# A recurrent block and a rounded feed-forward layer on one core: rounding of weights by adding transfers, maxima taken later, transfers in the planner

## What is computed

```
u = layernorm(x) @ W_in.T + b_in                      # 512 -> 1024
s[t] = tanh(u[t] + s[t-1] * gamma + beta)             # 1024 steps, one after another
x = x + layernorm(s @ W_out.T + b_out)                # 1024 -> 512
h = layernorm(x)
q(w) = w.astype(float8_e4m3fn).astype(float32)
gate = silu((h @ q(gate_w)) * gate_scale)             # 512 -> 1536
up = (h @ q(up_w)) * up_scale
x = x + layernorm(((gate * up) @ q(down_w)) * down_scale)   # 1536 -> 512
```

## Time and profile before

| | us |
|---|---|
| median of 3 runs | 600.39 (599.93 to 606.07) |
| the profiled execution | 603.18 |
| its span, first to last instruction | 601.4 |
| first scan starts | 21.07 |
| last scan starts | 539.14 |
| busy: PE, DVE, ACT, POOL | 557.9, 398.2, 325.5, 208.7 |

### The profile page before, as it was taken

How to read it: one execution, slowest core, us unless ns; L and a number is a source line. 1 busy time by engine, 2 the same in 40 slices (tenths; PEclk the granted TensorE clock), 3 DMA queues, 4 the chain that set the end, 5 groups by cost and what they waited for, 6 DMA issues and landing times.

```text
span 601.4 us, 10100 instructions
## 1 busy us (share of the span) xinstructions
PE 557.9 (93%) x2984; PEld 467.4 (78%) x2984; DVE 398.2 (66%) x1638; ACT 325.5 (54%) x1496; POOL 208.7 (35%) x335
## 2 busy tenths in 40 slices
PE   4999798899899999999999999999999997988993
PEld 4766465789779887988788988988798786876992
DVE  3987967778686666766685758665666677655213
ACT  2765564655557554755466545755575555551330
POOL 1100214356637232534244314432233233521622
PEclk9999899899999999999999999999999998999998
DMA  8774114001012001010012001200010000200000
GB/s 267 212 243 143 53 44 150 1 19 36 1 36 71 1 1 36 14 58 2 1 36 71 1 1 36 71 2 1 1 41 32 1 1 2 71 1 1 37 0 35
DMA packets 16598, 27.47 MB, mean 46 GB/s; under 512 B 2336, under 2 KB 4512, under 8 KB 16544
## 3 DMA queue, kind: packets, MB, share of 16 engines
q1 hardware_dynamic: 16544, 26.84, 13.9%
HBM read 22.63 MB, written 4.19 MB: 45 GB/s over the span
## 4 chain that ended last, share of the span: by engine, by line
DVE 35%; PE 32%; ACT 21%; issue 5%; DMA 4%; POOL 1%; SPq 1%; POOLq 0%; DVEq 0%; ACTq 0%
DVE recur L934 17%; ACT pairs L1215 12%; PE gate_up L854 11%; PE wide L811 6%; DVE fused L1050 5%; PE wide L880 4%; ACT pairs L1202 4%; PE wide L789 4%; ACT gated L1238 3%; PE wide L765 3%; ACT fused_hi L1254 2%; PE wide L898 1%; DVE x_norm L1024 1%; DVE z L1062 1%; DVE y L974 1%
## 5 line engine op out<-in xcount | busy, mean ns | idle before, releaser
L934 DVE TENSOR_TENSOR_SCAN recur<-recur,pairs 128x32 f32<-128x32 f32 x1024 | 235.7, 230 | 139.8 <-ACT pairs L1215 139.5
L1215 ACT ACTIVATE pairs<-recur 128x16 f32<-128x16 f32 x1024 | 191.8, 187 | 211.3 <-DVE recur L934 206.6
L811 PE MATMUL wide<-w_out_sb,pairs 128*128 128x512 f32 x256 | 116.0, 607 | 10.0 <-ACT pairs L1215 9.8
L1325 POOL TENSOR_TENSOR fused_lo<-fused,fused_hi 128x256 fp32r<-128x256 f32 x96 | 72.0, 750 | 145.6 <-ACT fused_hi L1254 145.5
L811 PEld LDWEIGHTS wide<-w_out_sb,pairs 128*128 128x128 f32 x256 | 74.7, 298 | 44.4 <-ACT pairs L1215 9.5
L789 PE MATMUL wide<-x_norm_t,w_in_sb 128*128 128x256 f32 x448 | 102.7, 386 | 6.3 <-ACT x_norm_t L1170 3.2
L854 PE MATMUL gate_up<-x_hi,gate_q 128*128 128x256 f32 x384 | 103.3, 301 | 4.4 <-DVE x_lo L1035 4.4
L789 PEld LDWEIGHTS wide<-x_norm_t,w_in_sb 128*128 128x128 f32 x448 | 85.1, 193 | 21.8 <-ACT x_norm_t L1170 6.3
L854 PE MATMUL gate_up<-x_lo,up_q 128*128 128x256 f32 x384 | 97.3, 286 | 0.0
L854 PE MATMUL gate_up<-x_hi,up_q 128*128 128x256 f32 x384 | 96.9, 285 | 0.0
L854 PE MATMUL gate_up<-x_lo,gate_q 128*128 128x256 f32 x384 | 96.5, 284 | 0.0
(11 more groups left out here) (93 smaller groups left out, 563.7 us busy)
## 6 DMA issues: line engine op xcount, KB each, us to landing
x_in<-x SPq DMA_DIRECT2D x16, 256.0 KB, 3.2
x_res<-x SPq DMA_DIRECT2D x16, 256.0 KB, 3.3
out<-z SPq DMA_DIRECT2D x14, 256.0 KB, 3.6
w_in_sb<-w_in_t SPq DMA_DIRECT2D x4, 512.0 KB, 5.6
w_out_sb<-w_out_t SPq DMA_DIRECT2D x8, 256.0 KB, 5.1
raw_own<-gate_w SPq DMA_DIRECT2D x6, 256.0 KB, 5.9
raw_own<-up_w SPq DMA_DIRECT2D x6, 256.0 KB, 4.2
z<-down_w SPq DMA_DIRECT2D x6, 256.0 KB, 3.0
```

Of the source, the lines that this page charges most:

```text
L811: ins = eng.matmul(wide[b][:, :], pairs_by_batch[:, state_slots(n, b), :, j, 0].rearrange("p s b -> p (s b)"), w_out_sb[:, j, :], start=(j ...
L934: eng.tensor_tensor_scan(preact.rearrange("p c k -> p (c k)"), factors.rearrange("p c k -> p (c k)"), pairs[:, (t - 1) % RING, :, :].rearr ...
L1215: eng.activation(pairs[:, t % RING, :, 0], preact[:, :, 1], ACT.Tanh).then_inc(s_state, 1)
L1325: eng.tensor_tensor(fused_lo[:, f, :], fused[:, f, :], fused_hi[:, f, :].bitcast(F32), ALU.subtract).then_inc(s_fused_lo, 1)
```

## The change

- The planner gets a fifth resource, `dma`, on which loads of pieces, of x, of the scale rows and of W_out take their turn (1.5 steps per 256 KB, landing 7 steps later). `ENGINE_FREE` says from when each resource is free; conversions of all 36 pieces are planned, none by hand.
- Twelve pieces (9, 13, 17, 21 and 28 to 35) are rounded by transfers that add: POOL issues one that adds the constants to the raw row, ACT writes the negated constants into the weight's place (`negate_constants`, two halves), and POOL issues a second that adds the raw row to it. The other 24 go through PE as before. POOL itself adds nothing any more.
- The maxima are taken of the rounded pieces, planned from step 60 on and at the lowest rank.
- Early pieces have nine raw rows (two of `x1_norm` more) and six rows of constants (two in `x1_lo`).
- In the head PE makes 4 products of zeros once DVE has cleared two rows of `fused`; the first u goes to four banks in parts of two columns of 128, and each part is copied by itself.

```diff
+ISSUE_STEPS, LOAD_STEPS, LOAD_LANDS = 1.0, 1.5, 7.0
+ADD_ISSUE_STEPS, SETTLE_ISSUE_STEPS, SUM_STEPS, SUM_LANDS = 2.2, 1.9, 3.0, 6.0
+ENGINE_FREE = {"tensor": -4.0, "vector": -18.0, "scalar": -1.5, "gpsimd": -20.0, "sync": -24.0, "dma": -9.5}
+DOWN_RANK, NEGATE_RANK, ISSUE_RANK, PEAK_RANK, FIRST_X1_RANK = 20.0, 0.0, -2.0, 150.0, -4.0
+PEAKS_FROM = 60.0
+WARM_PRODUCTS = 4
...
+def by_transfer(i):
+    return i >= 28 or i in (9, 13, 17, 21)
...
+    def load(name, after, parts=1):
+        t.add("sync", name, ISSUE_STEPS * parts, after, 0.0)
+        t.add("dma", ("landed", *name), LOAD_STEPS * parts, [(name, 0.0)], 0.0)
+        return [(("landed", *name), LOAD_LANDS)]
...
+            side("vector", ("constant", i), [(("power", i), 0.0)] + (unrounded(j) if j is not None else []), k - 1,
+                 two_ports=True)
+            if by_transfer(i):
+                for h in range(2):
+                    side("scalar", ("negate", i, h), [(("constant", i), 0.2)] + behind("negate", ("negate", i, h)),
+                         NEGATE_RANK + 0.01 * i)
+                t.add("gpsimd", ("add", i), ADD_ISSUE_STEPS,
+                      [(("constant", i), 0.2)] + behind("add", ("add", i)), ISSUE_RANK, no_ports=True)
+                t.add("dma", ("summed", i), SUM_STEPS, [(("add", i), 0.0)], 0.0)
+                t.add("gpsimd", ("settle", i), SETTLE_ISSUE_STEPS,
+                      [(("summed", i), SUM_LANDS)] + [(v, 0.2) for v in pair("negate", i)]
+                      + behind("settle", ("settle", i)), ISSUE_RANK, no_ports=True)
+                t.add("dma", ("settled", i), SUM_STEPS, [(("settle", i), 0.0)], 0.0)
...
             for h in range(2):
+                side("vector", ("peak", i, h), done(i) + behind("peak", ("peak", i, h)) + [(peaks_from, 0.0)], PEAK_RANK + 0.01 * i)
...
         raw = [raw_own[:, r, :] for r in range(OWN)] + [z[:, b, :] for b in range(batch)] + [
-            x_res[1][:, b, :] for b in range(batch)]
+            x_res[1][:, b, :] for b in range(batch)] + [x1_norm[:, b, :] for b in range(batch)]
+        rounders = [rounders_own[:, r, :] for r in range(NR)] + [
+            x1_lo[:, b * KD // 2:(b + 1) * KD // 2, :].rearrange("p k t -> p (k t)") for b in range(batch)]
...
-        for i in range(FIRST_PIECES):
-            at["raw", i] = HEAD + 20 + i
-            at["power", i] = HEAD + FIRST["pieces"] + 4 * i
...
+                eng.wait_ge(s_blank, 1)
+                for _ in range(WARM_PRODUCTS):
+                    eng.matmul(round_banks[0], fused[:, 0, 0:P], fused[:, 0:2, :].rearrange("p f t -> p (f t)"),
+                               start=True, stop=True)
...
+                for m in range(MS):
+                    yield HEAD + FIRST["first_u"][m]
+                    if m == 0:
+                        eng.wait_ge(s_x_norm_t, 1)
+                    eng.wait_ge(s_w_in_in[m], 16)
+                    for jj in range(2):
+                        j = 2 * m + jj
+                        for k in range(KD):
+                            ins = eng.matmul(wide[m][:, jj * P:(jj + 1) * P],
+                                             w_in_sb[:, k, j * P:(j + 1) * P], x_norm_t[:, k, 0:P],
+                                             start=(k == 0), stop=(k == KD - 1))
+                    ins.then_inc(s_u_psum, 1)
...
+                        wait_constant_read(eng, before)
...
+                        eng.mul(pieces[i][1][:, halves(h)], rounders[rounder_of[i]][:, halves(h)].bitcast(F32),
+                                -1.0).then_inc(s_negated, 1)
...
+                    yield at["add", i]
+                    eng.wait_ge(s_raw_in[raw_of[i]], 16 * (raw_use[i] + 1))
+                    eng.wait_ge(s_constant, i + 1)
+                    eng.dma_start(raw[raw_of[i]], rounders[rounder_of[i]].bitcast(F32),
+                                  accum_op=ALU.add).then_inc(s_summed[raw_of[i]], 16)
...
+                    yield at["settle", i]
+                    eng.wait_ge(s_negated, 2 * transfer_pieces(i + 1))
+                    eng.wait_ge(s_summed[raw_of[i]], 16 * sums_into_raw(i))
+                    eng.dma_start(pieces[i][1], raw[raw_of[i]], accum_op=ALU.add).then_inc(s_settled[raw_of[i]], 16)
```

More of the change, by code:

```diff
@@ L75, in lay @@
     def lay(self):
[L78 removed]
+        open_jobs = {e: [] for e in ENGINE_FREE}
         for name, job in self.jobs.items():
@@ L88, in lay @@
         begin, running = {}, []
-        free = {e: -60.0 for e in open_jobs}
+        free = dict(ENGINE_FREE)
         shared_until, pool_until = -60.0, -60.0
@@ L266, in converted, with read, unrounded @@
+    def read(i):
+        return [(("settled", i), SUM_LANDS)] if by_transfer(i) else [(("round", i), 0.3)]
+    def unrounded(i):
+        if by_transfer(i):
+            return [(("summed", i), SUM_LANDS)] + [(v, 0.2) for v in pair("negate", i)]
+        return [(("round", i), 0.3)]
     def converted(pieces):
[L267 removed]
+        return [v for i in pieces for v in done(i)]
     def weights():
[L271 to L296 removed]
@@ L297, in weights @@
[L297 to L310, removed]
@@ L311, in weights, with behind @@
-        for step in range(4):
-            before = [("peak", i, h) for i in range(FIRST_PIECES, NP) for h in range(2)] if step == 0 else [("guard", step - 1)]
-            side("vector", ("guard", step), [(v, 0.0) for v in before] +
-                 ([(v, 0.3) for v in done(NP - 1)] if step == 3 else []), 180)
+        before = {}
+        def behind(strand, name):
+            after = [(before[strand], 0.0)] if strand in before else []
+            before[strand] = name
+            return after
@@ new lines, in weights @@
+        for step in range(4):
+            after = [(v, 0.0) for v in pair("peak", NP - 1)] if step == 0 else [(("guard", step - 1), 0.0)]
+            side("vector", ("guard", step), after + (done(NP - 1) if step == 3 else []), PEAK_RANK)
+    x_landed = {1: load(("x_load", 1), [(-18.0, 0.0)], parts=batch)}
+    rows_landed = load(("rows",), [(2.0, 0.0)], parts=3)
+    w_out_landed = []
+    for j in range(KH):
+        w_out_landed += load(("w_out", j), [(W_OUT_FROM + W_OUT_EVERY * j, 0.0)])
@@ L331, in next_x @@
     def next_x(n):
-        norm_x(n, [(("t1", n - 1, b), 8.0) for b in range(batch)], rank(n - 1, 10) if n > 2 else X2)
+        x_landed[n] = load(("x_load", n), [(("t1", n - 1, b), X_BEHIND if n < 4 else 0.3) for b in range(batch)], parts=batch)
+        norm_x(n, x_landed[n], rank(n - 1, 10) if n > 2 else X2)
     next_x(2)
@@ L368, in timetable @@
             if p == 0 and i == 2:
-                after += converted(i for i in range(NP) if not by_pool(i))
+                after += converted(i for i in range(NP) if not by_transfer(i))
             for b in range(batch):
```

263 lines of the change are left out of this document (151 added, 112 removed).

## The result

The changed kernel takes 586.1 us (585.0 to 586.5, 4 runs) where the kernel before took 600.6. In a second comparison of five rounds it took 585.7 against 601.9, ratio 0.9735 (0.9702 to 0.9769). So it is 14.5 to 16 us faster where 9.2 was forecast. The direction was right and the three waits went as forecast.

The account below looks back on a forecast made before the run. The chain of scan and tanh was taken to bound the kernel, with PE close behind. Terms -9.2 - 1.1 + 2.0 - 0.9 = -9.2 us gave 594.0 us for the profiled execution, 591.2 for the median, range 586 to 601.

Parts of the forecast that it names:

- the three waits: DVE's waits for raw rows, 2.10 and 3.36 us for gate_w, 3.74 us for down_w; all taken as gone.
- The bound: Whole kernel: the chain of scan and tanh sets the end, with PE close behind; tail of 62 us untouched.
- The waits for loads: DVE's early scans: planning loads with more lead removes all three waits for raw rows, -9.2 us, bounds 0 and -9.2.
- The maxima: 72 operations of 0.39 us leave DVE's fullest stretch and fit free places among later scans; cost 0.
- The adds: Adding transfers: DVE's constants wait for adds to land, 0.5 us for each of four early pieces, +2.0 us.
- adds late: Rival: adds land 12.8 us from issue, DVE waits for constants' rows, 21 us on top, 610 us; chance 0.10.
- POOL can't issue: Rival: DVE's conversions shut out POOL's issues, four full waits on the path, 27.6 us, 617 us; chance 0.05.
- PE's roundings: PE does 24 roundings instead of 26, 2.6 us less work, given no term in the sum.
- The head: Before the first scan: ACT's last copies of the first u, two columns instead of four, take half, -0.9 us.
- the conversions' move out of the head: Masks and constants of pieces 0 to 4 on DVE begin with the scans instead of before the first; cost 0.
- the zeros' term: Zero products in PE's head, to have its clock up: taken as 0, bounds 0 and -1.8 us.
- The lock: DVE mask beside a POOL sum took 1.54 us instead of 0.43; with POOL's sums gone, -1.1 us.

Follow-up runs that it names:

- the pair in the planner: Kernel before with loads of raw rows planned as there 8 steps after issue and maxima late, of the rounded pieces: ratio 0.9816, 11.1 us saved.
- the four early transfers: Changed kernel with pieces 9, 13, 17 and 21 rounded by PE instead of by transfer: ratio 0.9787, 2.9 us above the changed kernel's median.

## Why the forecast had the sign and missed the size

- **The bound** was read rightly. PE still waits for the scans at the last product, and the tail is the same 62.3 us. The forecast's own test for it, the last scan at about 530, gave 522.
- **The waits for loads**, -9.2: the three holes are gone, 9.4 us above the usual steps. But "the planner counts loads" didn't buy that by itself. In the kernel before it gives 3.6 us.
- **The maxima**, costed at 0: this step of the mechanism failed. I counted free places from 60 us on and found that the moved ones fit, and took a full DVE ahead of that for a thing without a price. The price is that a job of another kind that stands behind them, here the copy of y, comes later, and PE and ACT with it. Put back early, the maxima cost 9.0 us in the changed kernel. In the kernel before, moving them gives nothing alone and 7.5 us once the loads are planned (11.1 - 3.6). The two parts aren't terms of a sum. That the waits came out at 9.4 where 9.2 was forecast is luck in part: the term held only because the maxima were moved with the loads' planning.
- **The adds**, +2.0: this term failed, measured 0. Its premise was that a row is wanted 6.6 us after an issue, at PE's pace. The adds of pieces 9 and 13 took 5.7 and 7.5 us, the second longer than 6.6. The constants that reuse their rows (pieces 15 and 19) were made only 8.9 and 16.6 us after the issues, so DVE never stood before such a row. Even with the adds unplanned the early four cost nothing. The rivals "adds late" and "POOL can't issue" are both out for the kernel as it is planned: an issue at 44 us took 0.86 us beside a DVE operation that makes constants, and with the adds unplanned one at 95 us took 0.86 with no DVE operation beside it. So no lock of the size of the earlier trace rows is seen on an issue. The longest of the three shown took 0.23 us more than that.
- **PE's roundings**: I had two fewer as off the path. Four more early ones cost 2.9 us, of which 1.4 show by step 256, so they may lie on it in part.
- **The head**, -0.9: this term failed, measured -3.0. The transposes and the first products took 1.8 us less (1.4 of it the products, 8.74 - 7.31), where I took 0 for the zeros. The copies gave 0.8, as costed. The last 0.4 is the mask of piece 5 that no longer stands ahead of the first scan. I had the conversions' move out of the head at 0, since DVE had nothing else to do there, and overlooked that the first scan stands behind them. With the zeros this matters more, as the kernel before with zeros shows: its first scan stood behind DVE for 1.8 us. The input to the zeros' term was wrong too. I had them end some 3 us before x. A product of 512 columns in float32 takes two records, so four took 6.04 us and ended 0.56 us ahead of the transposes. My argument that a gap of 3 us would lose their gain wasn't tested, since two zeros never brought the faster pace.
- **The lock**, -1.1: measured -1.2, the part of the hole after step 177 that is above the usual step.
- What was in no step: 3.4 us in all of small holes, 1.2 of them between steps 64 and 131, 0.6 to step 256, 1.6 behind it. The last is no more than the scatter of that stretch. For the others no run tells the cause.

In the profiled pair the miss of 7.8 us (17.0 where 9.2 was forecast) is thus 2.0 from the adds, 2.1 from the head, 0.3 from the waits and the lock, and 3.4 in no term. The parts of the whole can't be added from the experiments: the pair in the planner gave 11.1 us in the kernel before, the four early transfers 2.9 in the changed one, the zeros 1.9 and 2.8 in the one and the other, with wide intervals. What stays open is how the nine rows (4.9 us when taken away) divide with the maxima, since all of them act on the same hole after step 93, and what the zeros are worth in the whole.

## What to carry to other kernels

Where engines run a planned order, price a moved job by what the queue's other jobs gain in time, not only by whether it still fits where it goes. Two edits that relieve the same queue are to be tried together before either is dropped. Ask also what stands on every engine ahead of the first step of a chain: zeros that sped up PE by 2 us brought the first scan only 0.7 us forward where DVE's own queue stood before it. And work that is to bring an engine's clock up has to last until the faster pace has shown in its records; here half of it was worth nothing.

## What was not expected of the hardware

An adding transfer of 256 KB within SBUF landed after a median of 4.5 to 4.9 us from its issue (single ones 3.2 to 7.5), about as long as a load of as much from HBM in the same run (4.3 for rows of gate_w, 2.9 for rows of down_w), though it reads two operands. The Trainium skill (Collectives: The Full Stack, section "Stop ④ — SDMA + CCE: where bytes move and the add happens") has the add done in the transfer's data path. No run here shows where, and the landing time doesn't speak against it.

The granted clock doesn't always show PE's pace. It read 1.00 over the first 20 us of the kernel before, of the changed one and of it with two zeros and with none, while transposes ran at 0.28 us each in some and 0.16 in others. And one and the same place, the u products behind a gap of 1.94 to 1.97 us, met the faster pace in some executions (7.14 us) and a mix of both in others (8.83 us, granted clock 0.79).
